# Attention with a Mamba-2 layer behind it: the rows' maxima one bank of 512 columns a step, the second residual at step 19, x1's transposes at step 3

## What is computed

```
q = wq x + bq   (32 x 4096)      k = wk x + bk   (32 x 4096)      v = wv x + bv   (256 x 4096)
attn = softmax(q^T k, over the 4096 keys)
x1 = gamma * (v attn^T) + x
u  = layernorm over channels(x1)
z, xBC, dt = in_w u ;  xBC = silu(conv of 4 taps(xBC)) ;  dt = softplus(dt + dt_bias)
state_t = state_(t-1) * exp(-dt_t exp(A_log)) + dt_t x_t B_t^T ;  y_t = state_t C_t + Dp x_t
out = out_w rmsnorm(y * silu(z))
result = x1 + out * sigmoid(gate from the mean of out over positions)
```

## Time and profile before

| | us |
|---|---|
| median of 3 runs (3151.14 to 3154.02) | 3153.75 |
| the profiled execution | 3150.87 |
| its span, first to last instruction | 3148.7 |
| TensorE busy (21208 matmuls) | 2980.0 (95%) |
| VectorE busy (3417 instructions) | 2032.0 (65%) |
| ScalarE busy (3742) | 1930.0 (61%) |
| GpSimd busy (3087) | 2009.9 (64%) |

### The profile page before, as it was taken

One profiled execution on the slowest core, in us unless ns is written; L12 is line 12 of the kernel. 1 busy time (PEld: TensorE's weight loads), 2 busy tenths in 40 slices (PEclk: granted clock), 3 DMA queues, 4 the chain that ended last, 5 costly groups with the idle time before them and its releaser, 6 DMA issues. The chain is left out here.

```text
span 3148.7 us, 63156 instructions
## 1 busy us (share of the span) xinstructions
PE 2980.0 (95%) x21208; PEld 2322.5 (74%) x21208; DVE 2032.0 (65%) x3417; ACT 1930.0 (61%) x3742; POOL 2009.9 (64%) x3087
## 2 busy tenths in 40 slices
PE   6899999999999999999999999999999999999984
PEld 3767777777777777777777777777777777777762
DVE  5556666666666676676676666676666667666654
ACT  2565666666656566666665666666666666666652
POOL 2446666667756576666676656666676667777753
PEclk9999999999999999999999999999999999999986
DMA  3111111111311121222221222122221111212121
GB/s 123 49 37 46 44 51 58 31 54 49 103 63 65 58 71 58 91 77 74 82 77 38 72 76 72 62 76 69 65 89 36 43 49 55 69 50 69 42 95 67
DMA packets 101970, 200.99 MB, mean 64 GB/s; under 512 B 18480, under 2 KB 41392, under 8 KB 97264
## 3 DMA queue, kind: packets, MB, share of 16 engines
q1 hardware_dynamic: 98192, 195.08, 18.6%
q10 hardware_dynamic: 3456, 1.86, 0.2%
HBM read 131.21 MB, written 64.75 MB: 62 GB/s over the span
## 5 line engine op out<-in xcount | busy, mean ns | idle before, releaser
L723 POOL TENSOR_TENSOR p_lo<-p,p_hi 128x512 f16<-128x512 f32 x1024 | 1221.9, 1201 | 845.6 <-ACT p_hi L886 711.9
L879 ACT ACTIVATE p<-p_et 128x512 f32<-128x512 f32 x1024 | 612.2, 598 | 637.4 <-PE p_et L1138 598.0
L1156 PE MATMUL acc<-v_hi,p_hi 128*128 128x257 f16 x4096 | 954.3, 273 | 4.0 <-DVE work L1464 3.8
L1158 PE MATMUL acc<-v_lo,p_hi 128*128 128x256 f16 x4096 | 951.8, 272 | 0.0
L1420 DVE TENSOR_REDUCE maxes<-p_mx 128x1 f32<-128x1024 f32 x508 | 620.1, 1221 | 489.1 <-PE p_mx L1117 488.7
L886 ACT ACTIVATE p_hi<-p 128x512 f16<-128x512 f32 x1024 | 643.5, 629 | 10.0
L1164 PE MATMUL acc<-v_hi,p_lo 128*128 128x257 f16 x4096 | 622.8, 274 | 15.1 <-POOL p_lo L723 15.1
L1156 PEld LDWEIGHTS acc<-v_hi,p_hi 128*128 128x128 f16 x4096 | 399.3, 97 | 125.0 <-issue 54.8
L1158 PEld LDWEIGHTS acc<-v_lo,p_hi 128*128 128x128 f16 x4096 | 400.6, 98 | 117.8 <-issue 49.9
L1164 PEld LDWEIGHTS acc<-v_hi,p_lo 128*128 128x128 f16 x4096 | 399.9, 98 | 68.0 <-POOL p_lo L723 15.9
L1138 PE MATMUL p_et<-qs,kst 98*128 98x256 f16 x2048 | 393.3, 273 | 11.6 <-ACT p L879 11.1
(11 more groups left out here) (213 smaller groups left out, 4164.2 us busy)
## 6 DMA issues: line engine op xcount, KB each, us to landing
work<-rows_d SPq DMA_DIRECT2D x32, 1024.0 KB, 5.2
xin<-in_x_dram SPq DMA_DIRECT2D x48, 512.0 KB, 4.7
xr<-in_x_dram SPq DMA_DIRECT2D x32, 512.0 KB, 3.8
x_d<-x1c SPq DMA_DIRECT2D x31, 512.0 KB, 2.9
og_d<-og SPq DMA_DIRECT2D x29, 512.0 KB, 2.7
mix_x<-x_d SPq DMA_DIRECT2D x25, 512.0 KB, 4.7
mix_o<-og_d SPq DMA_DIRECT2D x24, 512.0 KB, 5.5
out_dram<-mix_o SPq DMA_DIRECT2D x24, 512.0 KB, 2.8
```

Source lines behind the costliest of these rows:

```text
L723: e.tensor_tensor(p_lo[:, n % RING, :], p32[:, n % P32S, :], p_hi[:, n % RING, :], ALU.subtract).then_inc(lo_pool, 1)
L879: e.activation(p32[:, n % P32S, :], p_et[:, :], ACT.Exp).then_inc(exp_done, 1)
L1156: e.matmul(acc[:, t, 0:C + 1], p_hi[:, r, at:at + P], v_hi[:, 2 * k + kk, 0:C + 1], start=(k == 0 and kk == 0), stop=False)
L1158: e.matmul(acc[:, t, 0:C], p_hi[:, r, at:at + P], v_lo[:, 2 * k + kk, :], start=False, stop=False, skip_group_check=True)
```

## The change

The unit of the maxima becomes a tile of one bank (128 queries x 512 keys) in place of a pair of banks. `tiles_at` gives one tile to every step, odd ones too, in place of a pair to every even step; in half block 0 a pair's two tiles stand at the same step as before. TensorE's `max_tile` issues one matmul and waits until the reduction of the tile two places before is done (four places in the part ahead of the loop, where acc's banks are used too); VectorE's `max_tile` reduces 512 columns. The matmuls are the same 1024, the reductions become 1024 in place of 512. K_XT becomes (13, 19): the residual's second transposes, ScalarE's copy of them and SP's load of the next xr move. K_X1T becomes 3: x1's transposes, ScalarE's copies into x1c and SP's store of x1c move one step back, behind cb of step 2.

```diff
--- before.py
+++ after.py
@@ -47,7 +47,7 @@
 
 
 
-K_X1T, K_UT, K_DT, K_DAT, K_CUM, K_YT, K_OUT = 2, 9, 10, 21, 23, 30, 0
+K_X1T, K_UT, K_DT, K_DAT, K_CUM, K_YT, K_OUT = 3, 9, 10, 21, 23, 30, 0
 K_U = (6, 7)
 K_XBC = (11, 16, 21, 26)
 K_Z = (22, 24)
@@ -57,7 +57,7 @@
 K_Y = (4, 8, 12, 17)
 K_SUM = (6, 10, 14, 19)
 K_SQ = (8, 12, 16, 21)
-K_XT = (13, 30)
+K_XT = (13, 19)
 K_XB = 4
 K_RMS = 22
 K_YN = (27, 28)
@@ -179,27 +179,22 @@
 assert len(PLACE) == len(FILLS)
 
 
-def pairs_at(h, k):
-
-    if h:
-        return [of] if (of := tiles_at(h, k)) is not None else []
-    early = {8: 0, 10: 1, 12: 2, 13: 3, 14: 4}
-    return [(1, k)] if k < PAIRS else [(2, early[k])] if k in early else []
-
-
 def tiles_at(h, k):
 
-    if k % 2:
-        return None
-    of = (h + 1, (k + AHEAD) // 2) if k < STEPS - AHEAD else (h + 2, (k - (STEPS - AHEAD)) // 2)
-    return of if of[0] < NHALF else None
-
-
-MAXIMA = [(0, n) for n in range(PAIRS)]
+
+    if h == 0:
+        early = {8: 0, 10: 1, 12: 2, 13: 3, 14: 4}
+        of = (1, 2 * k) if k < PAIRS else (2, 2 * early[k]) if k in early else None
+        return [of, (of[0], of[1] + 1)] if of else []
+    of = (h + 1, k + AHEAD) if k < STEPS - AHEAD else (h + 2, k - (STEPS - AHEAD))
+    return [of] if of[0] < NHALF else []
+
+
+MAXIMA = [(0, n) for n in range(STEPS)]
 for _n in range(NT):
-    MAXIMA += pairs_at(*divmod(_n, STEPS))
+    MAXIMA += tiles_at(*divmod(_n, STEPS))
 PLACE_MX = {of: n for n, of in enumerate(MAXIMA)}
-assert len(PLACE_MX) == NHALF * PAIRS
+assert len(PLACE_MX) == NHALF * STEPS
 
 
 def conv_attention_mamba_kernel(nc, x, wqkT, bqk, wvT, wv, gamma, inT, wqk, conv_w, conv_b,
@@ -225,7 +220,7 @@
         p32 = sb("p32", [P, P32S, BLK])
         p_hi = sb("p_hi", [P, RING, BLK], F16)
         p_lo = sb("p_lo", [P, RING, BLK], F16)
-        maxes = sb("maxes", [P, 2, 2, NB // 2])
+        maxes = sb("maxes", [P, 2, 2, NB])
         mcol = sb("mcol", [P, 2, 2])
         mparts = sb("mparts", [P, 2, 2, 2], F16)
 
@@ -486,9 +481,9 @@
                 "se2": (gate_raw, g + 1),
             }[name]
 
-        def mx_banks(h, n):
-
-            return p_mx if h or not n % 2 else acc
+        def mx_bank(h, n):
+
+            return (acc if not h and n % 4 > 1 else p_mx)[:, PLACE_MX[h, n] % 2, :]
 
         def conv_bank(g, m):
 
@@ -1103,20 +1098,17 @@
                                       wvT_sb[:, h, :], start=(h == 0), stop=(h == CH - 1))
                 mm.then_inc(filled, 1)
 
-            def max_pair(h, n):
-                wait(e, max_done, PLACE_MX[h, n] - (not h))
+            def max_tile(h, n):
+                wait(e, max_done, PLACE_MX[h, n] - (1 if h else 3))
                 if n == 0:
                     e.wait_ge(q_loaded[h % QS], 48 * (h // QS + 1))
                     if h % HB == 0 and h:
                         e.wait_ge(k_loaded, 48 * (h // HB))
-                if not h and n in (0, PAIRS // 4):
-                    e.wait_ge(k0_loaded[n // (PAIRS // 4)], 48)
-                t, pair = divmod(n, NB // 2)
-                for r in range(2):
-                    kb = 2 * pair + r
-                    mm = e.matmul(mx_banks(h, n)[:, r, :], qs[h % QS][0:STK, t * P:(t + 1) * P],
-                                  kst[h // HB % 2][0:STK, kb * BLK:(kb + 1) * BLK], start=True, stop=True)
-                mm.then_inc(mx_ready, 1)
+                if not h and n in (0, NB // 2):
+                    e.wait_ge(k0_loaded[n // (NB // 2)], 48)
+                t, kb = divmod(n, NB)
+                e.matmul(mx_bank(h, n), qs[h % QS][0:STK, t * P:(t + 1) * P],
+                         kst[h // HB % 2][0:STK, kb * BLK:(kb + 1) * BLK], start=True, stop=True).then_inc(mx_ready, 1)
 
             def max_rows(h):
                 o = begin(("mr", h, 0))
@@ -1272,7 +1264,7 @@
                 if g < G - 1 or not m:
                     wait(e, silu_done, g * CM + m)
                 else:
-                    e.wait_ge(*((exp_done, NT) if m == 1 else (max_done, NHALF * PAIRS)))
+                    e.wait_ge(*((exp_done, NT) if m == 1 else (max_done, NHALF * STEPS)))
                 for h in range(CH):
                     mm = e.matmul(conv_bank(g, m), inT_sb[:, h, C + m * P:C + (m + 1) * P], uT[:, h, :],
                                   start=(h == 0), stop=(h == CH - 1))
@@ -1282,8 +1274,8 @@
                 n = s * SLOT + K
                 if s < G:
                     energies(n + 3)
-                    for of in pairs_at(*divmod(n, STEPS)):
-                        max_pair(*of)
+                    for of in tiles_at(*divmod(n, STEPS)):
+                        max_tile(*of)
                 if s == 1 and K == 0:
                     e.wait_ge(w2_loaded, 16 * len(w_later))
                 for key in fills_at(s, K):
@@ -1302,11 +1294,11 @@
             values_of(0, 0, 1)
 
             e.wait_ge(qkf_done, NB)
-            for n in range(PAIRS):
-                max_pair(0, n)
-                if n == PAIRS // 2:
+            for n in range(STEPS):
+                max_tile(0, n)
+                if n == STEPS // 2:
                     values_of(0, 1, 0)
-                if n == PAIRS - 2:
+                if n == STEPS - 4:
                     values_of(0, 1, 1)
             e.wait_ge(ident_ready, 2)
             max_rows(0)
@@ -1414,10 +1406,10 @@
                 v.scalar_tensor_tensor(lo, bank(("v", b * NB + j, t))[:, :].rearrange("p (n c) -> p n c", n=2),
                                        scs[:, b % 2, 0:1], hi, ALU.mult, ALU.subtract).then_inc(v_lo_done, 1)
 
-            def max_pair(h, n):
-                t, pair = divmod(n, NB // 2)
+            def max_tile(h, n):
+                t, kb = divmod(n, NB)
                 e.wait_ge(mx_ready, PLACE_MX[h, n] + 1)
-                v.tensor_reduce(maxes[:, h % 2, t, pair:pair + 1], mx_banks(h, n)[:, :, :], AX.XY, ALU.max).then_inc(max_done, 1)
+                v.tensor_reduce(maxes[:, h % 2, t, kb:kb + 1], mx_bank(h, n), AX.X, ALU.max).then_inc(max_done, 1)
 
             def max_parts(h):
                 r = h % 2
```

## The result

| | before | after |
|---|---|---|
| median, us | 3153.48 | 3271.42 (3268.08 to 3274.20) |
| ratio, 95% interval | | 1.038 (1.0364 to 1.0395) |
| span of the profiled execution | 3148.7 | 3272.1 |

What follows compares the result with a forecast made beforehand. TensorE, busy 2797.81 of 2874.40 us, was taken to bound the kernel. Terms -12 -1 -3 -11 +59 +26 +2 +8 +1 = +69 us on 3150.87 gave 3220, 3223 for the median, stated as 3222; range 3198 to 3248.

Steps and rivals of the forecast that it cites:

- The sign and the main mechanism: Slower, chance 0.89; the second x1T fill at step 3 waits for VectorE's late mt: +59 us (+28 to +80).
- (b): Step 2: the cb product's wait for x1c goes, 30 x 0.41 = -12 us; only -1 us entered the sum.
- the clock: After holes of 2.4 us TensorE's clock halves in one slot in six: +8 us (0 to +48).
- step 16: `attended` stands behind one more reduction and TensorE waits for it: +2 us (0 to +9).
- step 8: The state product's wait for GpSimd, 21 times, is absorbed if TensorE comes later: up to -11 us, summed as -11.
- The reductions: VectorE: 512 columns take 0.69 us (0.61 to 0.75); 77 us more VectorE time, hidden on the whole.
- step 9: The cast into qs behind the maximum delays the second uT fill, 0.95 us in 27 slots: +26 us (+19 to +30).
- R3: Rival, chance 0.10: the clock falls in nearly every slot after the new hole; +109 us, 3263 us.
- The collision: Step 1's scan meets GpSimd's work on p_lo: 0.13 us a slot counted, up to 0.9 us more possible.
- R1: Rival, chance 0.16: smaller waits, VectorE's block of step 1 is 1.0 us shorter and the clock holds; +35 us, 3189 us.
- R2: Rival, chance 0.09: faster, mt and the cast come before TensorE reaches x1T and uT; -26 us, 3128 us.
- R4: Rival without its own chance: no two maxima delay TensorE in a step, nothing to spread; own part 0 to +3 us.

## Why the prediction was wrong, point by point

**The sign and the main mechanism were right.** VectorE's block behind the maximum of step 1, and x1T in cb's bank behind mt: 8.85 us from step 1 to step 4 against 8.87, +57.4 us against +58 (59 less the 1 of (b)). The kernel with x1T back at 2 and the one with the odd reductions at the end of the step show it. But the table's places add up to 124.8 us, and the forecast's terms for them to 68. Of the 57 us between them 24 are the clock, 21 step 16, and 8 step 8. At step 16 the path was wrong; at the other two the size was.

**The reductions** were 0.69 us as taken, and **step 9** held, 30.5 us against 26, and the cast ahead of the maximum takes all of it away.

**The failed step: step 16.** I put the price of one more reduction ahead of step 16 at +2 us and named `attended` as the one who stands behind it. It was +23.2. I had followed only those who stand behind VectorE on TensorE. The wait runs over ScalarE: the tap of step 13, the tanh that waits for it, and the exponentials queued behind the tanh. The row for it was there in the trace of before: ScalarE's tanh already waited for VectorE's taps 55 times, 45.3 us in all (81.7 after), and 31 of these waits, 35.0 us, were for the tap of step 13 (64.2 us after). The forecast's own rule, who waits for the instruction that is pushed back and what is queued behind the one who waits, was not applied a second time.

**The term of wrong size: the clock.** +8 us (5 of 28 slots) against +32.4. In the main part of the span the granted clock falls 21 times, 5 times before; 13 of the new ones come at step 3, and with x1T back at 2 there are 6 in all. Of the other 8, three follow TensorE's waits for p_lo at step 3, as before, three follow holes of 2.1 us at step 16 (two of 2.6 us before), and two follow holes of 2.6 us at step 8. Three falls, one each in slots 5, 6 and 14:

```profile
555.80:559.20 3.40, 3.40 (x16) 2.73 (x14) 0.69 (x1) 2.29 (x5) 2.22 (x10) 0.50 0.76 237
654.80:658.20 3.40, 3.40 (x15) 2.54 (x14) 0.69 (x1) 2.04 (x5) 2.08 (x11) 0.50 0.66 197
1446.80:1450.10 3.30, 3.30 (x17) 2.35 (x16) 0.00 (x0) 1.11 (x2) 1.82 (x10) 0.50 0.39 159
```

The two rows that I had, one fall in two holes of 2.4 us, said one in two; I took one in six without a reason in the rows. 28 x 1/2 x 1.7 = +24 would have been what they give, and the forecast 3239. R3, by which the clock falls in nearly every slot, was too high in its clock term (+48); the measured time is above its 3263 because step 16 and step 8 come on top.

**Taken off too much: step 8.** -11 us forecast for GpSimd's wait, which did go (14.4 us of holes to 0.4). But mr behind it waits for yt, 20.2 us instead of 9.5. yt follows the y fill of the same step, and when the state product no longer waits, TensorE comes to mr too early: a hole of 0.52 us in nearly every slot, and of 2.6 us in two. In the two kernels with xw first, where VectorE's program is that of before, the holes at mr are the same, 19 to 20 us. So a hole behind the one that goes was left out of the term, and most of the -11 us could not be had.

**The collision** of the scan with GpSimd's work didn't happen at step 1: 1.22 us, as before. It is GpSimd's xsd that was slowed down, 1.59 us instead of 0.61. It happened at step 13, 1.94 us (1.22 before), where it helped to make the tap late.

**Two rules of the Trainium skill.** The Trainium skill, "SBUF — State Buffer", section "Who interferes with whom", says that a VectorE instruction with two SBUF inputs contends with GpSimd's reads and that tensor_reduce doesn't. The traces agree, with scans of 1.22 and 1.94 us in the kernel after and reductions of 0.65 to 0.69 throughout; but the prediction concluded that the scan would pay at its new place, and at step 1 GpSimd paid. The Trainium skill, "TensorE: Matmul & The Clock Gate", section "A second HAM failure mode: psum-queue depth-cycling", tells of a kernel that cycles through PSUM banks, idles between groups of matmuls, and whose clock swings: not here. The kernel with the maxima alone changes the bank in every step, and its clock falls 4 times in the main part, against 5 before. The falls that the change adds follow the holes at steps 3, 8 and 16.

**The rivals.** R1 (smaller waits) and R2 (faster, no wait for mt) are out; R4's point, that no step had two maxima in TensorE's way, agrees with the runs: with the odd reductions last, one bank a step gives 3138.0, and pairs with the same moves 3136.2, so spreading the maxima wins nothing that can be measured.

## What to carry to other kernels

Splitting a batch of work that sits in every second step over all steps ties the consuming engine to the producer twice as often: everything behind the new wait in its program loses its lead. Before such a split, list for each odd step what the engine did ahead of time, who waits for that, and what is queued behind the one who waits, over all engines and not only the one that bounds the kernel; then put the new piece at the end of the step. And look behind each hole that goes: of a gain ahead of a place where the bound engine waits for another one, a part is given back there (6.8 of 15.5 us here), and a wait that goes can uncover the next one (mr behind the state product).

## What the runs showed of the hardware

A hole of some 2.4 us on TensorE, which recurs in each slot, costs more than its length. In the kernel after, 13 of its 28 such holes at step 3 were followed by a stretch at half the clock, of 3.4 us in all but two cases (10.2 us), and so were in the kernel with the cast ahead 18 of 28. The holes of 1.1 us at step 9, 30 times in the kernel after, never were; but in other kernels here single falls also followed holes of 1.1 to 1.7 us at step 8. The count changes between kernels whose step 3 is the same, so one trace gives the cost of such a hole only roughly.
